# A transformer stack on one core: the first pass of attention scores fills two neighbouring PSUM banks, and one maximum reads both

## The chip, the cores and the metric

The kernel runs on one core of one Trainium2 chip. The metric is the device time of one execution in microseconds (us). Engines are named as in the profile: PE is TensorE (PEld its weight loads), DVE is VectorE, ACT is ScalarE, POOL is GpSimd and SP is SyncE, which issues most DMAs. PSUM is where PE leaves its results; this kernel treats it as eight banks of 512 float32 columns in 128 partitions.

## The reference

Four transformer layers run over 4 batches of 512 tokens with 288 channels. Each has 16 attention heads of width 18 and a feed-forward part of width 1152; layer 0 has four experts, with two chosen for each token. Cut to attention and the order of the layers:

```python
def _attention(h, W_qkv, b_qkv, W_proj, b_proj):
    qkv = h @ W_qkv + b_qkv
    q, k, v = ...                      # 16 heads of 18
    attn = softmax(einsum('blhd,bmhd->bhlm', q * scale, k), axis=-1)
    o = einsum('bhlm,bmhd->blhd', attn, v).reshape(b, l, c)
    return o @ W_proj + b_proj
...
x = x + gate_msa * _attention(modulate(layernorm(x)))
x = x + gate_mlp * mlp(modulate(layernorm(x)))
```

The softmax is computed against the maximum of each row of scores. So every score is computed twice: a first pass with queries in the rows, from which only the row maxima are kept, and a second pass with keys in the rows, into which the negated maxima enter as two more rows of the contraction.

## The kernel before

A planner (`plan`) writes one list of steps for all engines; each engine's program walks the list and executes its own part of every step. So the order of work on each engine is the order of the list. `pe[0]` is the planner's own clock: each `put` adds the estimate of its kind from `PE_NS` (a step `s1` counts 230), and side work is woven in when that clock has moved on by a set amount.

The list has 16 stages of attention (batch b of layer L is i = 4L + b), and the feed-forward part of stage i - 1 follows the attention of stage i. Layer 2 groups its attention another way (`s1b`, `s2b`), which the change does not touch. In the other twelve stages:

- `s1_steps(i)` is the first pass. For each of 8 head pairs p and 4 query tiles q it puts two steps `s1` (x = 0 and 1: one matmul each, weights from partitions 64x to 64x + 53, 512 key columns, into a bank of its own), then two steps `s1_max`, one DVE reduction per bank. That is 8 * 4 * 2 * 12 = 768 matmuls (line L1737) and 768 reductions (L1496). After every two head pairs `rows` turns the maxima (L1743), splits them on DVE (L1502, L1505) and stores them by DMA (L1111) for the second pass.
- `at_steps(i)` is the second pass. A step `s2` (L1750) fills a pair of banks (4 and 5, or 2 and 3) with two matmuls, and ACT reads each pair in one exponential of 1024 columns (L1345). `av` (L1760) multiplies with the values into bank 6.
- `s1_steps(i + 1)` is a stream. Part of it runs one call per step inside the attention of stage i, and the rest beside the feed-forward part, as a side of `weave`. Stage 0 has nothing to hide its own first pass behind: 16 head-pair tiles run before its first `s2`, and 2 or 1 more follow each later step until they are done.
- `mid(i)` is woven between the feed-forward tiles too: `turn_o` turns the attention output (three steps, L1693 and L1695; ACT copies it, then DVE takes the remainder, L1481 or L1484), `project` multiplies four token tiles (L1647 with weights WP; DVE reads the bank in L1571), and `turn_x` turns the normed rows (three steps, L1680 and L1682; ACT reads the bank twice or three times, DVE last in L1472 or L1475). `fc1` (L1856) and `fc2` (L1871) are the feed-forward matmuls and use banks 2, 3, 6 and 7, `hid` is the DVE part between them (L1626).

Banks. `ring()` hands out single banks in turn, from a tuple that depends on the place: `RING_A` = (0, 1, 7) in attention, `RING_B` = (0, 1, 4, 5) beside the feed-forward part, `RING_0` = (0, ..., 5) for a short while after the attention of stage 0. The steps `s1`, `rows`, `turn_o`, `turn_x`, `project`, the query and key projection and the turned output in attention all draw from the same ring. `pair(k)` claims banks k and k + 1 together. On PE `may_fill(bk, n)` waits until the earlier content of the bank has been read: it waits for a semaphore that the reader of the bank raises. If the bank belonged to a pair, it waits for the reader of the pair.

`weave` beside the feed-forward part: in layer 0 at most one `s1` tile per 5000 of the planner's clock; in the six stages i = 5, 6 and 11 to 14 one after 400, so one after nearly every feed-forward step (one `fc1` tile or two `fc2`), and `mid` steps after 800, so a turn or a projection between any two such tiles for as long as `mid` has steps.

Of the kernel before, what the change touches and what calls it, by code (L numbers as in the profile page):

```python
# [11 lines left out]
AX = mybir.AxisListType  # L12
# [43 lines left out]
def r(ap):  # L56
    return ap.bitcast(F32R)


def view(ap, part, free, dims):  # L60

    step = ap.ap[0][0]
    return bass.AP(ap.tensor, ap.offset + part * step + free,
                   [[s * step if isp else s, n] for s, n, isp in dims])
# [14 lines left out]
def plan(full, s_av, s_tn, s_fc2, s_qw):  # L79
# [8 lines left out]
    def put(*a):  # L88
        steps.append(a)
        pe[0] += PE_NS.get(a[0], 0)  # L90
# [20 lines left out]
    def bank(k):  # L111
        settle(k)
        fills[k] += 1
        if in_pair[k]:
            other[k, fills[k] - 1] = (k - 1, in_pair[k])
        return (k, fills[k] - 1)
# [10 lines left out]
    ring_of, ring_n = [RING_0], [0]  # L127

    def ring():
        ring_n[0] += 1  # L130
        return bank(ring_of[0][ring_n[0] % len(ring_of[0])])

    jobs = [("ada", 0, 0), ("q", 0), ("v", 0), ("ada", 0, 1), ("ada", 0, 2), ("wg",), ("p", 0)]
    jobs += [("f", k) for k in range(3)]
# [183 lines left out]
    n_qt, qw, qk_n = [0], [0, 0, 0], [0, 0, 0]  # L318
# [88 lines left out]
    def s1_steps(i):  # L407
        def rows(g, last):
            bk = ring()
            put("rows", i, g, bk, last, m2_wait[0])  # L410
            m_n[g] += 4 * 16
            m2_wait[0] = (g, m_n[g])
            mrow[g] = m_n[g]
            s1_at[0] = (i, g)

        late = None
        for p in range(H // 2):
            g = p // 2
            for q in range(QT):
                while not hurry[0] and pe[0] < qk_at.get((i, min(g, 2)), 1e9) + QK_LAND:  # L420
                    yield
                bks = []
                for x in range(2):
                    bk = ring()
                    put("s1", i, p, q, x, bk, qk_n[min(g, 2)])
                    bks.append(bk)
                for x in range(2):
                    put("s1_max", p, q, x, bks[x])
                yield
                if late is not None and q == DEFER:  # L430
                    rows(*late)
                    late = None
                    yield
            if p % 2:
                late = (g, bk)
        yield
        rows(*late)
        yield
# [339 lines left out]
    for i in range(NI + 1):  # L778
        L, b = i // 4, i % 4
        if i < NI:  # L780
# [41 lines left out]
            m = mid(i)  # L822
# [26 lines left out]
def build(nc, x_in, cond, layers, gate_w, out):  # L849
    ctx = ExitStack()  # L850
    with ctx:
# [21 lines left out]
        QS = sb("QS", [128, 8, T])  # L873
        KS = sb("KS", [128, 8, T])
# [19 lines left out]
        MX = [sb(f"MX{n}", [128, 16]) for n in range(2)]  # L894
# [11 lines left out]
        PSA = ctx.enter_context(nc.psum_tensor("PSA", [128, 8 * 512], F32))  # L906
# [478 lines left out]
        def dve_program(e):  # L1385
# [3 lines left out]
            for kind, *a in steps:  # L1389
                if kind == "fix":  # L1390
                    key, k, m = a
# [98 lines left out]
                    e.tensor_tensor(r(HH[u][0:M, 1, :]), PS[bk][0:M, :], HH[u][0:M, 0, :],  # L1490
                                    ALU.subtract).then_inc(free[bk], 1)
                elif kind == "s1_max":
                    p, q, x, (bk, n) = a
                    col = 8 * x + 4 * (p % 2) + q
                    w.wait_ge(full[bk], n + 1)
                    e.reduce_max(MX[p // 2 % 2][:, col:col + 1], PS[bk][:, :], axis=AX.X).then_inc(free[bk], 1)  # L1496
                elif kind == "rows":
                    i, g, (bk, n), _, old = a
                    if old is not None:
# [129 lines left out]
        def pe_program(e):  # L1629
# [21 lines left out]
            for kind, *a in steps:  # L1651
# [79 lines left out]
                    token_rows(A[i % 2], [WV[:, 0, :], WV[:, 1, :]], [WVL[:, 0, :], WVL[:, 1, :]],  # L1731
                               WV[:, 2, :], q, bk).then_inc(full[bk], 1)
                elif kind == "s1":
                    i, p, q, x, (bk, n), land = a
                    w.wait_ge(s_qk[min(p // 2, 2)], land)
                    may_fill(bk, n)
                    e.matmul(PS[bk][:, :], r(QS[64 * x:64 * x + 54, p, q * 128:(q + 1) * 128]),  # L1737
                             r(KS[64 * x:64 * x + 54, p, :]), start=True, stop=True).then_inc(full[bk], 1)
                elif kind == "rows":
                    i, g, (bk, n), last, _ = a  # L1740
                    w.wait_ge(free[last[0]], last[1] + 1)
# [185 lines left out]
```

## Time and profile before

| | us |
|---|---|
| median of 3 runs | 2257.18 |
| lowest and highest | 2246.01 and 2261.70 |
| span of the profiled execution | 2257.0 |
| PE busy, DVE busy, ACT busy in it | 2033.0, 1335.6, 1143.6 |

The span is the time from the first to the last instruction of one profiled execution. Busy time is time in which the engine has an instruction in work, however slowly it proceeds: two matmuls that overlap count once, and a matmul at half the clock counts at its longer duration. A group of instructions is named by its line in the kernel and by out<-in. "Idle before" is the idle time of an engine just before the instructions of the group, with the engine whose instruction ended it.

### The profile page before, as it was taken

The page shows a single profiled execution, that of the slowest core. Times are in us where ns is not written, and L with a number is a line of the kernel's source. Part 1 is how long each engine was busy: PE and PEld are TensorE (multiplying, and loading weights), DVE is VectorE, ACT ScalarE, POOL GpSimd, SP SyncE. Part 2 cuts the span into 40 slices and gives each one's busy share as a digit, 9 for nine tenths or more (in the row PEclk, how much of TensorE's full clock was granted, in tenths as well). Part 3 has the DMA queues.
Part 4 walks back from the last instruction along what each step waited for, and adds up shares of the span by engine and source line. Part 5 has one row for each costly group of instructions (what it writes and reads, how often), then busy time and mean ns, then how long its engine had stood idle before and what let it go on. Part 6 is the DMA issues. An engine that isn't in the chain of part 4 may idle for free.

```text
span 2257.0 us, 38969 instructions
## 1 busy us (share of the span) xinstructions
PE 2033.0 (90%) x15592; PEld 1509.0 (67%) x15592; DVE 1335.6 (59%) x2940; ACT 1143.6 (51%) x1705; POOL 207.4 (9%) x311
## 2 busy tenths in 40 slices
PE   6978899899989998999799899899888898999898
PEld 4347388658966994788375657788786556464658
DVE  4757637756774767476556673462444849484833
ACT  2444624574655456445626464552443464637373
POOL 2000001202100211012010000011000000000001
PEclk9787989899989999999889999998898998999999
DMA  5333332343333233333322313346254141314011
GB/s 158 77 123 57 100 95 72 79 111 86 89 77 106 72 89 76 96 94 88 94 72 35 103 17 65 73 88 109 34 95 130 7 121 26 99 11 115 9 14 25
DMA packets 204731, 173.97 MB, mean 77 GB/s; under 512 B 54822, under 2 KB 164678, under 8 KB 204550
## 3 DMA queue, kind: packets, MB, share of 16 engines
q1 hardware_dynamic: 197974, 158.76, 30.1%
q0 software_dynamic: 6576, 12.71, 2.1%
q8 instruction: 124, 2.03, 0.4%
q14 instruction: 57, 0.47, 0.1%
HBM read 125.57 MB, written 40.11 MB: 73 GB/s over the span
## 4 chain that ended last, share of the span: by engine, by line
PE 63%; DVE 18%; ACT 12%; DMA 3%; issue 2%; SPq 2%; POOL 0%; ACTq 0%; POOLq 0%; DVEq 0%
PE PSA L1856 16%; PE PSA L1871 13%; DVE MX L1496 7%; PE PSA L1647 5%; PE PSA L1760 5%; PE PSA L1737 5%; ACT PB L1345 4%; PE PSA L1707 4%; PE PSA L1750 4%; PE PSA L1719 2%; DVE FL L1396 2%; PE PSA L1780 1%; ACT FH L1375 1%; PE PSA L1670 1%; DVE HH L1626 1%
## 5 line engine op out<-in xcount | busy, mean ns | idle before, releaser
L1496 DVE TENSOR_REDUCE MX<-PSA 128x1 f32<-128x512 f32 x768 | 490.4, 682 | 296.9 <-PE PSA L1737 293.2
L1856 PE MATMUL PSA<-A,FH 128*128 128x256 f32 x2520 | 445.3, 292 | 12.5 <-DVE HH L1626 9.6
L1871 PE MATMUL PSA<-FH,HH 128*128 128x288 f32 x2016 | 447.7, 313 | 2.0 <-DVE HH L1626 2.0
L1382 ACT ACTIVATE HH<-PSA 128x512 fp32r<-128x512 f32 x252 | 150.4, 597 | 572.5 <-PE PSA L1856 567.3
L1345 ACT ACTIVATE PB<-PSA 128x1024 f32<-128x1024 f32 x384 | 370.9, 1025 | 102.5 <-PE PSA L1750 101.8
L1856 PEld LDWEIGHTS PSA<-A,FH 128*128 128x128 f32 x2520 | 364.9, 195 | 34.6 <-issue 17.3
L1871 PEld LDWEIGHTS PSA<-FH,HH 128*128 128x128 f32 x2016 | 329.7, 195 | 42.3 <-issue 38.0
L1871 PE MATMUL PSA<-FL,HH 128*128 128x288 f32 x1008 | 303.7, 301 | 0.0
L1737 PE MATMUL PSA<-KS,QS 54*128 54x512 f32 x768 | 226.1, 517 | 40.0 <-DVE MX L1496 14.0
L1255 POOL TENSOR_TENSOR X<-X,TM 128x288 f32<-128x288 f32 x128 | 101.1, 808 | 1496.7 <-DVE TM L1561 1496.6
L1760 PE MATMUL PSA<-PB,VT 128*32 128x512 f32 x1536 | 219.6, 637 | 0.0
L1750 PE MATMUL PSA<-QS,KS 56*128 56x512 f32 x768 | 172.6, 498 | 51.2 <-ACT PB L1345 27.2
L1626 DVE TENSOR_TENSOR HH<-PSA,HH 128x512 fp32r<-128x512 f32 x252 | 171.8, 682 | 76.1 <-ACT PSA L1383 75.8
L1856 PE MATMUL PSA<-A,FL 128*128 128x256 f32 x1008 | 208.0, 288 | 6.3 <-DVE FL L1396 6.3
L1871 PEld LDWEIGHTS PSA<-FL,HH 128*128 128x128 f32 x1008 | 196.8, 195 | 0.0
L1750 PEld LDWEIGHTS PSA<-QS,KS 56*128 56x128 f32 x768 | 70.2, 198 | 165.4 <-ACT PB L1345 84.8
L1737 PEld LDWEIGHTS PSA<-KS,QS 54*128 54x128 f32 x768 | 94.3, 203 | 115.1 <-DVE MX L1496 37.8
L1856 PEld LDWEIGHTS PSA<-A,FL 128*128 128x128 f32 x1008 | 159.3, 195 | 10.3 <-DVE FL L1396 9.1
L1383 ACT ACTIVATE PSA<-PSA 128x512 f32<-128x512 f32 x252 | 149.5, 593 | 0.0
L1375 ACT CAST FH<-ST 128x672 fp32r<-128x672 f32 x171 | 123.2, 748 | 32.9 <-PE PSA L1871 13.5
L1396 DVE TENSOR_TENSOR FL<-ST,FH 128x544 fp32r<-128x544 f32 x171 | 125.3, 733 | 5.3
L1707 PE MATMUL PSA<-A,WQ 128*126 128x512 f32 (+1 forms) x300 | 95.5, 421 | 23.0 <-DVE HH L1490 9.5
(166 smaller groups left out, 2261.5 us busy)
## 6 DMA issues: line engine op xcount, KB each, us to landing
qkd<-HH SPq DMA_DIRECT2D x48, 504.0 KB
ST<-in_L_cond_w SPq DMA_DIRECT2D x51, 432.0 KB
ST<-in_L_cond_w SPq DMA_DIRECT2D x102, 192.0 KB
QS<-qkd SPq DMA_DIRECT2D x88, 144.0 KB
KS<-qkd SPq DMA_DIRECT2D x88, 144.0 KB
QS<-qkd SPq DMA_DIRECT2D x144, 72.0 KB
KS<-qkd SPq DMA_DIRECT2D x144, 72.0 KB
ST<-in_L_cond_w SPq DMA_DIRECT2D x153, 48.0 KB
```

The costliest lines, as they stand in the source:

```text
L1345: e.activation(pbf[st % 3][:, p * 1024:(p + 1) * 1024], PSA[:, bk * 512:(bk + 2) * 512], ACT.Exp, scale=SCALE).then_inc(free[bk], 1)
L1382: e.activation(r(HH[u][:, 0, :]), PS[bk][:, :], gelu)
L1383: e.activation(PS[bk][:, :], PS[bk][:, :], gelu).then_inc(s_gelu, 1)
L1396: e.tensor_tensor(r(lo), ST[k % 2][:, s0:s0 + nl], hi[:, 0:nl], ALU.subtract).then_inc(s_wlo, 1)
L1496: e.reduce_max(MX[p // 2 % 2][:, col:col + 1], PS[bk][:, :], axis=AX.X).then_inc(free[bk], 1)
L1626: e.tensor_tensor(r(HH[u][:, 1, :]), PS[bk][:, :], HH[u][:, 0, :], ALU.subtract).then_inc(free[bk], 1)
L1707: m = e.matmul(PS[bk][0:M, :], r(w_), r(x_), start=(z == 0), stop=(z == 6))
L1737: e.matmul(PS[bk][:, :], r(QS[64 * x:64 * x + 54, p, q * 128:(q + 1) * 128]), r(KS[64 * x:64 * x + 54, p, :]), start=True, stop=True).then ...
L1750: m = e.matmul(PS[bk + x][:, :], r(KS[64 * x:64 * x + 56, 2 * g + p, kt * 128:(kt + 1) * 128]), r(QS[64 * x:64 * x + 56, 2 * g + p, :]), s ...
L1760: m = e.matmul(PS[bk][32 * hh:32 * hh + 32, :], VT[:, kt, h * V1:h * V1 + 32], PB[st % 3][:, hh, :], start=(kt == 0), stop=(kt == 3))
L1856: m = e.matmul(PS[bk][:, s_ * 256:(s_ + 1) * 256], r(w_), r(x_[:, half * 256:(half + 1) * 256]), start=(z == 0), stop=(z == 6))
L1871: m = e.matmul(PS[bk][:, 0:C], r(HH[u][:, c, tk]), r(w_), start=False, stop=(j == NCH - 1 and z == 2))
```

## The change

In `s1_steps` the two matmuls of a tile no longer draw two banks one by one. A new `ring_pair()` walks the same ring until it meets an even bank followed by its neighbour, and claims both as a pair. One step `s1` then issues both matmuls after one wait and raises one semaphore behind the second. One step `s1_max` waits for it and reduces 2 x 512 columns in one DVE instruction, which writes the two maxima 8 columns apart. The columns of MX, the matmuls themselves and everything behind `rows` are as before. The planner now counts one `s1` where it counted two.

```diff
+    def ring_pair():
+        order = ring_of[0]
+        while True:
+            ring_n[0] += 1
+            k, k1 = order[ring_n[0] % len(order)], order[(ring_n[0] + 1) % len(order)]
+            if k % 2 == 0 and k1 == k + 1:
+                ring_n[0] += 1
+                return pair(k)
...
-                bks = []
-                for x in range(2):
-                    bk = ring()
-                    put("s1", i, p, q, x, bk, qk_n[min(g, 2)])
-                    bks.append(bk)
-                for x in range(2):
-                    put("s1_max", p, q, x, bks[x])
+                bk = ring_pair()
+                put("s1", i, p, q, bk, qk_n[min(g, 2)])
+                put("s1_max", p, q, bk)
...
-                    p, q, x, (bk, n) = a
-                    col = 8 * x + 4 * (p % 2) + q
+                    p, q, (bk, n) = a
+                    col = 4 * (p % 2) + q
                     w.wait_ge(full[bk], n + 1)
-                    e.reduce_max(MX[p // 2 % 2][:, col:col + 1], PS[bk][:, :], axis=AX.X).then_inc(free[bk], 1)
+                    e.reduce_max(view(MX[p // 2 % 2][:, :], 0, col, [(1, 128, True), (8, 2, False)]),
+                                 PSA[:, bk * 512:(bk + 2) * 512].rearrange("p (x n) -> p x n", x=2),
+                                 axis=AX.X).then_inc(free[bk], 1)
...
-                    i, p, q, x, (bk, n), land = a
+                    i, p, q, (bk, n), land = a
                     w.wait_ge(s_qk[min(p // 2, 2)], land)
                     may_fill(bk, n)
-                    e.matmul(PS[bk][:, :], r(QS[64 * x:64 * x + 54, p, q * 128:(q + 1) * 128]),
-                             r(KS[64 * x:64 * x + 54, p, :]), start=True, stop=True).then_inc(full[bk], 1)
+                    for x in range(2):
+                        m = e.matmul(PS[bk + x][:, :], r(QS[64 * x:64 * x + 54, p, q * 128:(q + 1) * 128]),
+                                     r(KS[64 * x:64 * x + 54, p, :]), start=True, stop=True)
+                    m.then_inc(full[bk], 1)
```

## Rows read from the trace of the kernel before

**Rows 1.** The page: span, busy time by engine, the chain that ended last by line

```profile
span 2257.0 us, 38969 instructions
PE 2033.0 (90%) x15592; PEld 1509.0 (67%) x15592; DVE 1335.6 (59%) x2940; ACT 1143.6 (51%) x1705; POOL 207.4 (9%) x311
PE PSA L1856 16%; PE PSA L1871 13%; DVE MX L1496 7%; PE PSA L1647 5%; PE PSA L1760 5%; PE PSA L1737 5%; ACT PB L1345 4%; PE PSA L1707 4%; PE PSA L1750 4%; PE PSA L1719 2%; DVE FL L1396 2%; PE PSA L1780 1%; ACT FH L1375 1%; PE PSA L1670 1%; DVE HH L1626 1%
```

**Rows 2.** The page's groups: busy us, mean ns | idle before, what ended it

```profile
L1496 DVE TENSOR_REDUCE MX<-PSA 128x1 f32<-128x512 f32 x768 | 490.4, 682 | 296.9 <-PE PSA L1737 293.2
L1345 ACT ACTIVATE PB<-PSA 128x1024 f32<-128x1024 f32 x384 | 370.9, 1025 | 102.5 <-PE PSA L1750 101.8
L1737 PE MATMUL PSA<-KS,QS 54*128 54x512 f32 x768 | 226.1, 517 | 40.0 <-DVE MX L1496 14.0
```

**Rows 3.** Idle PE and PEld before L1737, 0 to 200 us, by releaser (us, times)

```profile
  DVE MX L1496: 35.0, 62
```

**Rows 4.** The same from 200 us to the end

```profile
  DVE A L1472: 21.7, 25
  DVE MX L1496: 16.8, 26
  DVE A L1481: 16.5, 20
```

**Rows 5.** Busy time by stretch: PE, PEld, DVE, ACT, POOL; granted clock, DMA share, GB/s

```profile
50.00:62.00 12.00, 11.64 (x21) 5.40 (x21) 11.20 (x19) 0.00 (x0) 0.00 (x0) 0.50 0.70 202
```

**Rows 6.** Timeline of stage 0's first pass, half clock: start, length, instructions [idle before]

```profile
49.97 0.80 PE L1737 MATMUL PSA<-KS,QS 54*128 54x512 f32 x2 [3.35 <-DMA KS<-qkd]
...
50.80 12.05 DVE L1496 TENSOR_REDUCE MX<-PSA 128x1 f32<-128x512 f32 x20 [3.92 <-PE PSA L1737]
...
68.87 1.54 PE L1750 MATMUL PSA<-QS,KS 56*128 56x512 f32 x4
...
73.87 1.94 PE L1760 MATMUL PSA<-PB,VT 128*32 128x512 f32 x8
```

**Rows 7.** Timeline at full clock: a step with two tiles, then a tile alone

```profile
92.08 2.48 DVE L1496 TENSOR_REDUCE MX<-PSA 128x1 f32<-128x512 f32 x4
92.82 0.49 PE L1737 MATMUL PSA<-KS,QS 54*128 54x512 f32 x1 [0.76 <-DVE MX L1496]
93.24 1.06 PE L1760 MATMUL PSA<-PB,VT 128*32 128x512 f32 x8
...
153.70 0.50 PE L1737 MATMUL PSA<-KS,QS 54*128 54x512 f32 x2
```

**Rows 8.** Groups by shape on DVE: one operation at two lengths

```profile
L1396 DVE TENSOR_TENSOR FL<-ST,FH 128x544 fp32r<-128x544 f32 x171 | 125.3, 733 | 5.3
...
L1396 DVE TENSOR_TENSOR WQL<-ST,WQ 128x1152 fp32r<-128x1152 f32 x4 | 5.4, 1359 | 0.1
```

**Rows 9.** L1737 in the last of six dense stretches: PE, PEld, clock, DMA share, GB/s

```profile
2077.00:2135.00 58.00, 12.30 (x42) 4.74 (x42) 0.98 0.20 35
```

**Rows 10.** Timeline: projection, tile, maxima, next projection, DVE's read of the first

```profile
1863.57 0.69 PE L1647 MATMUL PSA<-WP,A 128*128 128x288 f32 x4
...
1864.58 0.51 PE L1737 MATMUL PSA<-KS,QS 54*128 54x512 f32 x2
...
1865.12 1.29 DVE L1496 TENSOR_REDUCE MX<-PSA 128x1 f32<-128x512 f32 x2 [0.47 <-PE PSA L1737]
...
1865.91 0.69 PE L1647 MATMUL PSA<-WP,A 128*128 128x288 f32 x4
...
1866.33 0.45 DVE L1571 TENSOR_TENSOR TD<-PSA,GB 128x288 f32<-128x288 f32 x1
```

**Rows 11.** Timeline: two turns of the attention output, and the tile behind the second

```profile
1850.68 0.60 PE L1693 MATMUL PSA<-ID,OT 128*128 128x128 f32 x4
1851.48 0.68 DVE L1481 TENSOR_TENSOR A<-PSA,A 128x512 fp32r<-128x512 f32 x1
1852.22 0.50 PE L1737 MATMUL PSA<-KS,QS 54*128 54x512 f32 x2 [0.94 <-DVE A L1481]
```

## The prediction

> **What bounds the kernel now.** I read the page first: busy times and the chain that ended last [rows 1]. PE is busy 2033.0 of 2257.0 us and DVE 1335.6, and the feed-forward lines L1856 and L1871 lead the chain. DVE's maxima still stand there with 7%. Then the groups [rows 2]: the 768 maxima cost DVE 490.4 us, and of the idle time of PE before the score matmuls (40.0 us) 14.0 us end with a maximum. So DVE as a whole is not the bound, and I have to see where PE waits for it. I asked the line L1737 for its releasers in two stretches. These counts add idle time of PE and of its weight loads, so they show where and not how much. Before 200 us maxima account for 35.0 us [rows 3]. In all the rest, more than 2000 us, they account for 16.8, and there the larger part is waits for reads of turned tiles (L1472 and L1481, 21.7 and 16.5) [rows 4]: a score matmul drew a bank that a turn had used just before. So two places matter: stage 0, whose own first pass hides behind nothing, and the six dense stages of the feed-forward part (i = 5, 6, 11 to 14), where tiles, turns and projections share one ring; the last of them is in [rows 9].
>
> **The price of one maximum.** The trace has no reduction over 1024 columns. The bound from below is the one over 512, 0.68 us [rows 2], and from above two of them, 1.36. One DVE operation at 544 and 1152 elements takes 0.733 and 1.359 us, 1.03 ns for each further element [rows 8]; so I take 0.682 + 512 * 0.00103 = 1.21 us. ACT's read of a pair points the same way: a single 1.025 us instruction reads two banks [rows 2]. Busy DVE time falls by 384 * (1.36 - 1.21) = 58 us. Where reductions follow each other they start 12.05 / 20 = 0.60 us apart [rows 6], so what DVE saves in its queue is 1.20 - (0.60 + 0.53) = 0.07 us per tile, not 0.15.
>
> **The price of one fill.** Two score matmuls use different halves of the rows and run side by side when both banks are free: two take 0.80 us at half clock [rows 6] and 0.50 us at full clock [rows 7], where one alone takes 0.49 [rows 7]. So issuing them together costs PE nothing, and it is what PE already does after 200 us.
>
> **The banks.** Here the change costs. RING_A = (0, 1, 7) holds only one even pair, so every tile in attention gets banks 0 and 1. The next tile cannot start until the maximum over both has ended. Three single banks become one buffer.
>
> *Stage 0, 16 tiles before the first s2.* They run at half the clock, 0.50 granted [rows 5]. Before, DVE is the bound at 2 * 0.60 = 1.20 us per tile, and the last fill is followed by s2 at 68.87 [rows 6]. After, a tile is a closed loop: 0.06 us from the release to the matmul (the first of four maxima ends at 92.76, the matmul starts at 92.82 [rows 7]), 0.80 for the fill, 0.03 to the start of the reduction (50.77 to 50.80 [rows 6]), 1.21: 2.10 us. Fifteen loops from 49.97 put s2 at 49.97 + 31.5 = 81.5 instead of 68.9: **+12.7 us**. Behind that s2 stand two tiles, s2, rows, one tile and av, which came 5.00 us after s2 [rows 6]. Now three loops (6.3) and 0.7 for the fill: **+2.0**.
>
> *Stage 0, five more steps with two tiles each.* The second tile waits for the maximum of the first: 92.08 + 1.21 + 0.06 = 93.35, and av follows 0.42 later as before, at 93.77 instead of 93.24 [rows 7]; 5 * 0.53 = **+2.7**. Nothing hides these 17 us. PE, DVE and then s2, ACT and av work in series there, and behind PE's waiting score matmul stand s2, av and the projections of the next stage. The SP queue is delayed with them, since its weight loads wait for DVE's splits, which stand in the same list.
>
> *Attention of later stages:* one tile per step. The loop at full clock is 0.06 + 0.50 + 0.03 + 1.21 = 1.80 us, and a step has two exponentials of 1.025 us [rows 2], so it fits: 0. The cover is ACT and PE together; gone, it would cost what stage 0 pays.
>
> *The dense stages.* RING_B = (0, 1, 4, 5) has two pairs, so tiles alone alternate and stay double-buffered. With a turn or projection between two tiles that ends. It takes, say, bank 4; ring_pair skips 5 and takes 0 and 1; the next single bank is 4 again. So each turn or projection waits for the read of the one before it, where until now they went round four banks. A projection starts at 1863.57, its tile 1.01 later, the maximum 0.54 after that, and DVE reads the projection (0.45 us, L1571) only behind the maximum, since its step comes later in the list [rows 10]. With 1.13 for the maximum in the queue and 0.06 to PE, the next one can start 1.01 + 0.54 + 1.13 + 0.45 + 0.06 = 3.19 us after the first. It started 2.34 after [rows 10]: +0.85. A stage has four such steps (three between projections, one to the rows step), one of them with a long fc1 between, which I count at half: 3.5 * 0.85 = 3.0. In the turns the wait exists already, one place later: the tile behind the second turn waits 0.94 us for L1481 [rows 11]. Now the turn itself would wait until 1851.48 + 0.68 + 0.06 = 1852.22, when the tile used to start; the tile comes one turn (0.60) later: +0.6, twice: 1.2. The turns of normed rows move in the same way, and there the waits of the tiles for L1472 fall away; I count 0 and bound it by another 1.2. A stage costs 3.0 + 1.2 = 4.2, six stages **+25**. From below it is 0, if DVE comes so much earlier that the next one is ready; from above 6 * 5.4 = 32.
>
> *The rest.* Layer 0's sparse stages have a long fc1 or four fc2 between such steps: 0. After the attention of stage 0 RING_0 has three pairs and DVE is the bound; by the code some 17 tiles * 0.07 = **-1**. In the dense stages DVE's backlog shrinks; what PE waits for maxima there is inside the 16.8 [rows 4], I take **-6** of it. The planner's clock, which counts a tile at 230 instead of 460, moves side work by at most a step or two: 0.
>
> A rule of the Trainium skill speaks for the change. VectorE: DVE Perf Modes, section on the TRN2 errata, says that a fixed latency is paid per instruction, so that "a single large tile pays it once". By the figures of its table (120 cycles plus the columns at 0.96 GHz) an estimate is 0.66 us for 512 columns and 1.19 for 1024. The trace agrees for the first (0.68); no run here shows the second.
>
> **The sum.** 2257.0 + 12.7 + 2.0 + 2.7 + 25 - 1 - 6 = 2292 us. The span of the profiled execution is the median of the runs (2257.18), so I leave it at that.
>
> **The rivals.**
> 1. *Only stage 0 pays.* The shared single bank in the dense stages is paid back by DVE's shorter queue. For: the last of these stretches has 42 score matmuls, 21 tiles, in 58 us [rows 9], so there is air between them. Against: the arithmetic of rows 10. Time: 2257 + 17 - 1 - 3 = 2270.
> 2. *Faster, or not slower: the DVE saving counts on the path.* Maxima are 7% of the chain, 158 us [rows 1]; at 1.21 instead of 1.36 that is 11% less, -17: 2240. For: the chain. Against: in stage 0, where these 7% mostly lie, the loop decides. It turns at a loop of 1.20 us; with 0.89 for release, fill and start the reduction would have to take 0.31, less than one over 512 columns. The skill's rule above is this rival.
> 3. *The clock falls more often.* The first pass of stage 0 ran at half clock with PE waiting between single fills [rows 5]. If the new short waits in the dense stages bring that state there, the fc1 and fc2 work of a few stretches takes twice its time; at 3 more us for each of the six stages on top of the forecast, 2292 + 18 = 2310. TensorE: Matmul & The Clock Gate, section on PSUM-queue depth-cycling, describes such a fall when PE idles briefly between groups of matmuls. The last dense stage, with 0.98 granted in spite of its waits [rows 9], speaks against it.
>
> **How the numbers follow.** Forecast (both places pay) 0.60, rival 1 0.22, rival 2 0.06, rival 3 0.12. The forecast's own range is 2277 to 2304: stage 0 between 13 and 20, dense stages between 12 and 32. The range for 8 in 10 reaches to rival 1 and rival 3: 2264 to 2314. One per cent is 22.6 us, about what a measurement of this kernel can tell from no change. Over 2279.8 lie rival 3 and nine tenths of the forecast, 0.66; rival 1, the rest of the forecast and most of rival 2 lie within 1%, 0.31; faster 0.03.
>
> **What the profile after would show.** The maximum as x384 at about 1210 ns. In stage 0 fills about 2.1 us apart, with PE waiting for MX, and the first s2 near 81.5 us. L1750 and L1760 shifted by 17 at the end of that attention. In the dense stages waits of L1647 for L1571 and of L1693 for L1481, which are not there now, and fewer waits of L1737 for L1481. Wrong I would be if the dense stages ran through as before (rival 1), if the reduction over two banks took under 1 us, or if something in stage 0 turned out to wait for a DMA that lands at the same time in both kernels.

## The result, and the profile after

| | before | after |
|---|---|---|
| median, us | 2259.44 | 2380.39 |
| lowest and highest | 2246.01 and 2262.40 | 2371.58 and 2382.43 |
| span of the profiled execution | 2257.0 | 2369.8 |

The changed kernel takes 1.054 times as long (95% interval 1.051 to 1.058): 121 us more, where 35 were forecast and 57 was the upper end of the range. The direction was right, the size off by more than three times.

Lines of the kernel after: the maximum is L1501 (L1496 before), the first-pass matmul L1745 (L1737), `rows` L1752 (L1743) with its DMA in L1116 (L1111), the second pass L1759 (L1750), `av` L1769 (L1760), the exponential L1350 (L1345), the projection L1654 (L1647) with its DVE reads in L1568 and L1578 (L1561, L1571), `turn_o` L1700 and L1702 with its DVE read in L1486, `turn_x` L1687 and L1689 with its DVE read in L1477, `fc1` L1865, `hid` L1633.

The page of the kernel after, the lines that answer to [rows 1] and [rows 2]:

```profile
span 2369.8 us, 38586 instructions
PE 2038.3 (86%) x15592; PEld 1501.3 (63%) x15592; DVE 1314.4 (55%) x2556; ACT 1147.0 (48%) x1705; POOL 207.3 (9%) x311
...
L1501 DVE TENSOR_REDUCE MX<-PSA 128x2 f32<-128x1024 f32 x384 | 467.8, 1220 | 344.7 <-PE PSA L1745 344.0
L1745 PE MATMUL PSA<-KS,QS 54*128 54x512 f32 x768 | 201.6, 521 | 72.9 <-DVE MX L1501 47.6
```

One maximum takes 1.220 us (1.21 forecast). DVE works 21 us less than before, PE 5 us more. Of the 113 us of span 107 are more idle time of PE. But the 5 us are the difference of two larger changes. The first-pass matmuls, which now always run side by side, fill 24.5 us less of PE's time (226.1 [rows 2] and 201.6). All its other instructions are the same as before and take longer: the time in which PE is busy with one of them is 1866 us before and 1892 after. The granted clock has two levels in both traces, 0.5 and 1.0. Its mean is 0.932 before and 0.917 after, and the time at 0.5 is 309 and 394 us. So some 25 us of the loss are work that takes longer, as it does at the lower clock, and the rest are waits. The trace of waits (idle time of PE in all, times, longest) names those, and they aren't in one place:

```profile
PE PSA L1745 <- DVE MX L1501: 47.6, 43, 2.9
PE PSA L1759 <- ACT PB L1350: 35.0, 38, 5.4
PE PSA L1759 <- DMA QS<-M: 18.3, 6, 6.0
PE PSA L1687 <- DVE A L1477: 14.7, 10, 2.6
PE PSA L1759 <- DVE MX L1501: 14.3, 8, 2.9
...
PE PSA L1654 <- DVE TD L1578: 10.2, 15, 1.6
```

Besides the waits for maxima there are two kinds that the forecast did not price where they came: the second pass of stage 0 waits for a DMA (`QS<-M`, the stored row maxima), and turns and projections wait for DVE's reads of the turn or projection before them.

Stage 0's first pass, from the timeline of PE (start, length, instructions, idle before): the fills, and the first `s2`.

```profile
79.97 0.80 PE L1745 MATMUL PSA<-KS,QS 54*128 54x512 f32 x2 [1.32 <-DVE MX L1501]
82.08 0.79 PE L1745 MATMUL PSA<-KS,QS 54*128 54x512 f32 x2 [1.32 <-DVE MX L1501]
82.67 1.06 PE L1759 MATMUL PSA<-QS,KS 56*128 56x512 f32 x4
```

Fills start 2.11 us apart (2.10 forecast), and the first `s2` stands at 82.67 instead of 68.87 [rows 6] (81.5 forecast). Then come the rows of the second and third group (PE's turn, its DMA on the SP queue, and the `s2` that needs it):

```profile
98.81 0.38 PE L1752 MATMUL PSA<-ID,MX 128*16 128x128 f32 x1
...
99.92 2.67 SPq L1116 DMA_DIRECT2D QS<-M  x4
...
105.23 1.22 PE L1759 MATMUL PSA<-QS,KS 56*128 56x512 f32 x4 [6.04 <-DMA QS<-M]
...
125.63 0.38 PE L1752 MATMUL PSA<-ID,MX 128*16 128x128 f32 x1
...
130.58 1.22 PE L1759 MATMUL PSA<-QS,KS 56*128 56x512 f32 x4 [4.57 <-DMA QS<-M]
```

From the turn to the `s2` it takes 6.4 and 5.0 us, and PE idles through 6.04 and 4.57 of it. In the kernel before, PE had other work between the two.

I split the 113 us at the first `s2` of each stage and at the first value projection behind its attention, so the attention of a stage and the feed-forward part beside it stand apart. Each kernel has one profiled execution. Two kernels that differ before the first `s2` alone (those of experiments 4 and 5) are up to 5 us apart in one of the later places, so a few us in one place say little. After less before, in us:

| | first `s2` | attention 0 | sparse: beside feed-forward of layer 0 (i = 1 to 4) | attention of 3 and 4 | dense: i = 5, 6, 11 to 14 | all the rest |
|---|---|---|---|---|---|---|
| forecast | 12.7 | 4.7 | 0 | 0 | 25 - 6 = 19 | -1 |
| measured | 13.8 | 23.0 | 34.2 | 11.1 | 22.9 | 7.8 |

The first and the dense part came near the forecast. 68 us came where the forecast had 4.7, 0 and 0. The time at half the clock grew from 41 to 85 us up to the end of attention 0 and from 35 to 64 us in the sparse stages; in the dense ones it was 63 us before and 55 after.

### The profile page after: what moved, and what is told of

Its sections match the earlier page's. It is cut to its first block, busy times and chain, and to the rows that moved or that the text cites. A ratio compares the mean times of both kernels' runs of the same rounds, so it can differ in the third digit from the quotient of the medians.

```text
span 2369.8 us, 38586 instructions
## 1 busy us (share of the span) xinstructions
PE 2038.3 (86%) x15592; PEld 1501.3 (63%) x15592; DVE 1314.4 (55%) x2556; ACT 1147.0 (48%) x1705; POOL 207.3 (9%) x311
## 4 chain that ended last, share of the span: by engine, by line
PE 59%; DVE 20%; ACT 13%; issue 3%; DMA 3%; SPq 2%; POOL 0%; ACTq 0%; POOLq 0%; DVEq 0%
PE PSA L1865 15%; PE PSA L1880 11%; DVE MX L1501 8%; PE PSA L1769 6%; PE PSA L1654 5%; PE PSA L1745 4%; PE PSA L1759 4%; PE PSA L1714 4%; ACT PB L1350 3%; DVE FL L1401 2%; ACT FH L1380 2%; PE PSA L1726 2%; DVE HH L1633 2%; PE PSA L1789 1%; ACT HH L1387 1%
## 5 line engine op out<-in xcount | busy, mean ns | idle before, releaser
L1501 DVE TENSOR_REDUCE MX<-PSA 128x2 f32<-128x1024 f32 x384 | 467.8, 1220 | 344.7 <-PE PSA L1745 344.0
L1865 PE MATMUL PSA<-A,FH 128*128 128x256 f32 x2520 | 447.7, 293 | 22.7 <-DVE HH L1633 12.5
L1350 ACT ACTIVATE PB<-PSA 128x1024 f32<-128x1024 f32 x384 | 370.5, 1023 | 143.8 <-PE PSA L1759 143.0
L1865 PEld LDWEIGHTS PSA<-A,FH 128*128 128x128 f32 x2520 | 366.1, 196 | 47.0 <-issue 21.7
L1745 PE MATMUL PSA<-KS,QS 54*128 54x512 f32 x768 | 201.6, 521 | 72.9 <-DVE MX L1501 47.6
L1759 PE MATMUL PSA<-QS,KS 56*128 56x512 f32 x768 | 175.1, 511 | 73.9 <-ACT PB L1350 35.0
L1769 PE MATMUL PSA<-PB,VT 128*32 128x512 f32 x1536 | 226.3, 654 | 0.3 <-ACT PB L1350 0.3
L1633 DVE TENSOR_TENSOR HH<-PSA,HH 128x512 fp32r<-128x512 f32 x252 | 171.7, 681 | 97.5 <-ACT PSA L1388 97.2
L1865 PE MATMUL PSA<-A,FL 128*128 128x256 f32 x1008 | 208.8, 289 | 5.2 <-DVE FL L1401 5.0
L1759 PEld LDWEIGHTS PSA<-QS,KS 56*128 56x128 f32 x768 | 70.9, 204 | 191.6 <-ACT PB L1350 87.5
L1745 PEld LDWEIGHTS PSA<-KS,QS 54*128 54x128 f32 x768 | 80.4, 205 | 139.8 <-DVE MX L1501 64.8
L1865 PEld LDWEIGHTS PSA<-A,FL 128*128 128x128 f32 x1008 | 160.0, 196 | 9.0 <-DVE FL L1401 8.0
L1380 ACT CAST FH<-ST 128x672 fp32r<-128x672 f32 x171 | 123.0, 748 | 24.5 <-PE PSA L1880 14.3
L1714 PE MATMUL PSA<-A,WQ 128*126 128x512 f32 (+1 forms) x300 | 95.7, 422 | 19.9 <-DVE HH L1495 8.2
```

Source lines behind the costliest of these rows:

```text
L1350: e.activation(pbf[st % 3][:, p * 1024:(p + 1) * 1024], PSA[:, bk * 512:(bk + 2) * 512], ACT.Exp, scale=SCALE).then_inc(free[bk], 1)
L1380: e.copy(r(hi), ST[k % 2][:, s0:s0 + nh]).then_inc(s_whi, 1)
L1501: e.reduce_max(view(MX[p // 2 % 2][:, :], 0, col, [(1, 128, True), (8, 2, False)]), PSA[:, bk * 512:(bk + 2) * 512].rearrange("p (x n) -> ...
L1633: e.tensor_tensor(r(HH[u][:, 1, :]), PS[bk][:, :], HH[u][:, 0, :], ALU.subtract).then_inc(free[bk], 1)
L1714: m = e.matmul(PS[bk][0:M, :], r(w_), r(x_), start=(z == 0), stop=(z == 6))
L1745: m = e.matmul(PS[bk + x][:, :], r(QS[64 * x:64 * x + 54, p, q * 128:(q + 1) * 128]), r(KS[64 * x:64 * x + 54, p, :]), start=True, stop=True)
```

## The experiments

In every one of them, "restored" or "halved" is the entry of a step `s1` in `PE_NS`, the planner's estimates. The kernel before takes between 2255.6 and 2259.4 us in all comparisons. Numbers for places are differences to the execution of [rows 1], divided as in the table above.

**1. The planner's clock alone, both ways.** A tile was two steps of 230 on the planner's clock and is now one of 230. One kernel is the changed one with the old cost per tile, the other is the kernel before with the new one.

```diff
 # the changed kernel:
-         "s1": 230,
+         "s1": 460,
```

> The changed kernel with the planner's count of a tile set back to its old sum (an s1 step counts 460, not 230), so that all work stands in the order of the kernel before and only the banks, the one semaphore and the one maximum are changed. Banks theory (the closed loop over one pair and turns and projections that fall on the same bank cost the time, the order costs nothing): as the changed kernel, 2370 to 2385. Clock theory (halving the count moved steps, above all the rows steps of stage 0, so that PE waits for their DMAs): the 16 us of waits of L1759 for QS<-M in stage 0's attention go and some of the waits in the sparse stages; 2340 to 2355 if it is half of the loss above my forecast, under 2300 if it is nearly all.

```diff
 # the kernel before:
-         "s1": 230,
+         "s1": 115,
```

> The kernel before with an s1 step counted 115 instead of 230, so a tile counts 230 as in the changed kernel: the order of work of the changed kernel, with the banks and maxima of before. Clock theory: slower by what the order costs, 15 to 40 us, with PE waiting for DMA QS<-M about 6 us twice in stage 0. Banks theory: within 5 us of before. If the two parts add, this run's loss and that of the run with the count restored sum to the 121 us of the change.

Measured: 2344.04 us with the clock restored (ratio 1.037, 1.034 to 1.040), 85 us over the kernel before. The clock alone: 2295.86 us (1.016, 1.013 to 1.019), 37 us over it. The two add up to 122, and the change cost 121. So the banks and the single maximum cost 85, and a number that no engine ever sees costs 37. With the clock alone, attention 0 is 21.9 us longer and the sparse stages 2, 3 and 4 lose 3.6, 6.4 and 2.9. The wait is the same as in the changed kernel:

```profile
109.91 0.28 PE L1743 MATMUL PSA<-ID,MX 128*16 128x128 f32 x1
...
115.68 1.22 PE L1750 MATMUL PSA<-QS,KS 56*128 56x512 f32 x4 [5.49 <-DMA QS<-M]
```

**2. Why the clock costs so much in stage 0.** `s1_steps` starts with a gate: the tiles of a group are not listed before the planner's clock has passed the time at which the group's queries and keys were asked for, by `QK_LAND` = 12000.

```python
                while not hurry[0] and pe[0] < qk_at.get((i, min(g, 2)), 1e9) + QK_LAND:
                    yield
```

With tiles at half the cost the planner's clock passes this mark later. In its list the first three steps of attention 0 get no tile, and the rows of the second and third group stand right ahead of the first `s2` of their group; in the kernel before two more steps of the attention lie between. The kernel here is the clock alone (as above), and stage 0 has no gate.

```diff
-                while not hurry[0] and pe[0] < ...
+                while i and not hurry[0] and pe[0] < ...
```

> The run with the clock alone changed, without the gate that holds back tiles of stage 0 until the planner's clock has passed a mark. Clock theory: the 21 us that stage 0's attention costs there come from this gate alone (tiles skipped in three steps, then rows steps right before the s2 that needs them), so they go: about 2275. What stays, 15 us in the sparse stages 2 to 4, comes from the places of turns and projections. If it stays at 2296, the gate is not the cause.

Measured: 2270.46 us (1.0075, 1.0046 to 1.0104), 25 us less than with the gate by the medians and 19 by the two ratios, and the waits of PE for `QS<-M` are 2.6 us in all (19.2 with the gate, 3.3 in the kernel before). Attention 0 takes 67.0 us, where it took 92.8 with the gate and 70.9 in the kernel before: the 21.9 us that the clock costs there are gone, and 4 more with them. So the gate in stage 0 is some 22 of the 37 us. (The kernel before without the gate was not run, so how much of the 4 us is this edit by itself is open.) The rest, about 15, stays in this kernel too, 10.5 of it in the sparse stages 2 to 4; which of the moved turns and projections makes it was not tried.

**3. The choice of banks alone.** The kernel before with its two semaphores and its two maxima, but the two banks of a tile are an even one and its neighbour, found by the same walk as `ring_pair`.

```diff
-                for x in range(2):
-                    bk = ring()
+                for x, k in enumerate(ring_two()):
+                    bk = bank(k)
```

> The kernel before, with its order, its two semaphores and its two maxima, but the two banks of a tile always drawn as an even bank and its neighbour, as the changed kernel draws them. Turns and projections then fall on the same bank as in the changed kernel, but each bank comes free by itself. If the shared bank of turns and projections is the cost, this is near the run with the clock restored, less only the longer loop of stage 0: there the loop per tile should be 0.06 + 0.80 + 0.03 + 0.68 = 1.57 us instead of 2.10, so 15 * 0.5 = 8 us and some 5 us in the steps with two tiles less. If the single maximum and semaphore are the cost, it is near before (2259).

Measured: 2355.82 us (1.042, 1.037 to 1.046), 97 us over the kernel before. The first `s2` is 3.8 us late and not 11.6, because here the next tile's first matmul waits for one maximum only. In attention 0, the sparse stages and attention 3 and 4 it is within 2 us of the changed kernel with the clock restored; it is worse in the dense stages (44 us lost against 32) and in all the rest (9 against -1). So the whole of the 85 us comes with the banks that a tile may take, and merging semaphore and maximum gives some 12 us back.

**4. The bank that has rested longest.** The changed kernel, clock restored, and both `ring` and `ring_pair` take the bank, or the pair, that was drawn longest ago, in place of the next one of the tuple.

```diff
-        return bank(ring_of[0][ring_n[0] % len(ring_of[0])])
+        k = min(ring_of[0], key=lambda k: (used[k], ring_of[0].index(k)))
+        used[k] = ring_n[0]
+        return bank(k)
...
-        while True:
-            ring_n[0] += 1
-            k, k1 = order[ring_n[0] % len(order)], order[(ring_n[0] + 1) % len(order)]
-            if k % 2 == 0 and k1 == k + 1:
-                ring_n[0] += 1
-                return pair(k)
+        k = min((k for k in order if k % 2 == 0 and k + 1 in order),
+                key=lambda k: max(used[k], used[k + 1]))
+        used[k] = used[k + 1] = ring_n[0]
+        return pair(k)
```

> The run with the clock restored, but single banks and pairs are drawn by longest time since use instead of by walking the ring, so that turns and projections alternate between two banks while tiles stay on the other pair. In attention nothing changes: tiles still have only banks 0 and 1. If the collisions of turns and projections are the cost outside stage 0, this falls to 2257 + 17 for stage 0 - 7 for DVE = about 2267, at most 2275. If it stays where the run with the clock restored is, the collisions are not the cost.

Measured: 2267.47 us (1.0036, 1.0019 to 1.0053). 77 of the 85 us are gone, with the same pairs and the same single maximum. Stage 0 has lost 20.3 us. Behind it every sparse and dense stage is faster than before or at most 2 us slower (the last three are faster by 3 to 5 us), and attention 3 and 4 are within 2. The waits of PE's projections for DVE's reads of the projection before (`TD`, 10.7 us with the clock restored) and of its turns for those of the turned attention output (14.7 us) are gone from the list. The planner's list shows why. In stage 2 the three turns and four projections draw banks 5, 4, 1, 0, 1, 0, 5 in the kernel before, 0, 0, 0, 0, 1, 0, 0 in the changed one with its clock restored, and 5, 4, 5, 4, 5, 4, 5 here. What is left is stage 0, where `RING_A` has one pair, whatever is chosen:

```profile
PE PSA L1747 <- DVE MX L1503: 49.5, 47, 2.3
```

**5. Three pairs for stage 0's first pass.** Banks 2 to 5 are idle until the first `s2`; a tile listed before it may take them.

```diff
-        order = ring_of[0]
+        order = ring_of[0] if s2_first[0] else RING_0
...
+                s2_first[0] = True          # at the first s2
```

> The run with least recently used banks, and until the first s2 of stage 0 the tiles may also use the pairs 2-3 and 4-5, which are idle then. Banks theory: the closed loop over one pair costs 12 us there; with three pairs DVE is the bound at 0.60 + 0.53 = 1.13 us per tile, the first s2 comes at 50 + 16 * 1.13 + 1 = 69 us instead of 81, and the total falls by 12 to about 2255. If the single reduction or the half clock were the cost there, the first s2 stays near 81.

Measured: 2254.83 us (0.9995, 0.9974 to 1.0016), 13 us less than the run before (9 by the two ratios). The first `s2` comes at 66.33 us (69 expected, 68.87 in the kernel before). On the timelines of PE and DVE tiles now start 1.13 us apart, and DVE is what they wait for:

```profile
52.18 0.80 PE L1749 MATMUL PSA<-KS,QS 54*128 54x512 f32 x2 [0.34 <-DVE MX L1505]
53.31 0.79 PE L1749 MATMUL PSA<-KS,QS 54*128 54x512 f32 x2 [0.34 <-DVE MX L1505]
...
48.63 11.41 DVE L1505 TENSOR_REDUCE MX<-PSA 128x2 f32<-128x1024 f32 x10 [1.62 <-PE PSA L1749]
```

Ten maxima in 11.41 us: 1.14 each, where ten tiles before took 12.05 [rows 6].

**6. The second tile behind `av`.** Where a step of attention 0 has two tiles, they share one pair, so `av` stood behind a matmul that waits for a maximum. The second tile now goes behind `av`.

```diff
-            for _ in range(2 if i == 0 else 1):
-                s1_step()
+            s1_step()
...
+            if i == 0 and st < 16:
+                s1_step()                   # behind av
```

> The run before, and in the attention of stage 0 the second tile of a step stands behind av instead of right behind the first, so that av's matmuls cover the maximum of the first tile. Banks theory: the wait of 1.3 us of the second tile (seven such steps) goes, 5 to 9 us less than the run with the wide first pass, about 2248, below the kernel before. If something else holds stage 0's steps (ACT, the DMAs of rows), no change against that run.

Measured: 2246.33 us (0.9959, 0.9939 to 0.998), 9 us under the kernel before in the same comparison. It is the fastest of all. Attention 0 takes 71.7 us, where it took 80.9 in the run before and 70.9 in the kernel before. Not all of these 9 us are the waits: in attention 0 the clock is at half for 17 us, against 38 in the run before, and PE is busy 7.7 us less with the same matmuls.

**7. What the single maximum is worth.** Two more kernels go back to two semaphores and two maxima of 512 columns, the banks still drawn as pairs that rested longest: once in the kernel before, and once with all placements of the fastest one.

> The kernel before with the banks drawn as in the run with least recently used banks (same order, same banks), but two semaphores and two maxima per tile. It tells what the single maximum gives when the banks are the same: by my count 0.07 us per tile wherever DVE is behind, so this is slower than the run with least recently used banks by 5 to 15 us in the dense stages, and faster by some 8 to 12 us in stage 0, where each bank comes free by itself; total 2262 to 2275.

> The kernel of the later second tile and the least recent banks, but each first-pass tile again with two semaphores and two maxima of 512 columns in place of one of 1024. Theory A (the single maximum itself is worth something where VectorE is the one behind): the 384 maxima cost 1.22 us each against 2 x 0.66 us, 0.10 us a tile, so at most 38 us of VectorE's time, of which the path sees a part: 2250 to 2262 us. Theory B (the placements and the bank choice made the whole gain, and the maximum nothing): 2246 us, as the kernel with the single maximum.

Measured: 2270.05 us (1.0058, 1.0033 to 1.0082), and 2260.20 us (1.0001, 0.9981 to 1.002). With the same order and banks as the fastest kernel, two maxima cost more than one: 14 us by the medians, 9 by the two ratios, each ratio uncertain by 4 to 5 us. Experiment 3 against the changed kernel with its clock restored gives 12. The first of the two kernels against experiment 4 gives only 3 (5 by the two ratios): two maxima are 11 us slower in the dense stages, but the first `s2` comes 7 us earlier, since there each bank comes free by itself, both near what was expected. So one semaphore and one maximum together are worth 3 to 14 us, by the kernel that they stand in, and 9 to 14 in the fastest. In the single executions of the two fastest kernels the difference sits in stage 0 (the first `s2` 2 us, its attention 1.6, the stretch behind it 3.5) and in the dense stages 12 to 14 (about 6), and the sparse stages go 4 us the other way. A part of it is the granted clock, which is at half for 284 us with one maximum and for 318 with two. What one maximum gives at the same clock was not separated.

**8. Are the reads late because they are listed late?** In the sparse stages of the changed kernel PE waits before turns and projections, though long `fc1` and `fc2` work stands between them. In stage 2 (540.5 to 708.6 us of the kernel after), the waits of PE:

```profile
...
PE PSA L1700 <- DVE A L1486: 2.7, 1, 2.7
PE PSA L1687 <- DVE A L1477: 2.5, 1, 2.5
PE PSA L1654 <- DVE TM L1568: 2.1, 1, 2.1
```

The last of them on the timeline: the projection is complete in its bank before 567, DVE reads it at 572.79, and the next projection starts 0.05 us after this read has ended.

```profile
566.22 0.30 PE L1654 MATMUL PSA<-WP,A 98*128 98x288 f32 x1
...
570.23 1.23 DVE L1501 TENSOR_REDUCE MX<-PSA 128x2 f32<-128x1024 f32 x1 [4.24 <-PE PSA L1745]
571.37 0.93 DVE L1568 SCALAR_TENSOR_TENSOR TM<-PSA,CW,GB 128x288 f32<-128x288 f32 x2
572.79 0.46 DVE L1568 SCALAR_TENSOR_TENSOR TM<-PSA,GB 128x288 f32<-128x288 f32 x1 [0.48 <-POOL X L1260]
...
573.30 1.33 PE L1654 MATMUL PSA<-WP,A 128*128 128x288 f32 x4 [2.13 <-DVE TM L1568]
```

In the code these reads are put with `later(...)`: they enter the list only when `mid` is taken up again, or when the bank is drawn again. That is right ahead of the next turn or projection, behind all the `hid` and maxima between. DVE was not busy all that time: it stood idle for 4.24 us ahead of the maximum that comes before the read in its list. The kernel with the clock restored, and the reads listed directly behind their matmuls:

```diff
-            later(bk[0], put, "turno_lo", c, slot, bk, n_o[0])
+            put("turno_lo", c, slot, bk, n_o[0])
...
-            later(bk[0], residual, i, q, bk, 0)
+            residual(i, q, bk, 0)
```

(and the same in both forms of `turn_x`)

> The changed kernel with the cost of the planner's clock restored, and with the VectorE and ScalarE reads of turns and projections listed directly behind their matmuls, not when the attention's chain is taken up again. Theory A (a read listed late makes the next turn or projection, which has the same bank, wait for it, whatever stands between): the sparse stages' 20 us of loss and a part of the dense ones' go, 2310 to 2330 us against 2344 us. Theory B (the read is slow in itself, and where it is listed changes nothing): 2344 us. Theory C (a read listed at once holds back the maxima or the copies behind it on VectorE and ScalarE): over 2350 us.

Measured: 2306.78 us (1.021, 1.018 to 1.025), 37 us less (36 by the two ratios). The sparse stages' loss goes from 19.9 to 5.2 us, the dense ones' from 32.2 to 13.1. In stage 2 PE no longer waits before a turn or a projection. But the same edit could be good by itself, so it was made in the kernel before and in the fastest kernel, where banks go round.

> The kernel before with the reads of turns and projections listed directly behind their matmuls, as the control of the same edit in the changed kernel, where it gave 37 us. Theory A (the late listing costs only together with the shared bank): within 6 us of the kernel before, 2252 to 2265 us. Theory B (it costs in any kernel of this shape): 2215 to 2235 us, and the 37 us then say nothing about the shared bank.

> The fastest kernel so far (least recent banks, wide first pass, second tile later) with the reads of turns and projections listed directly behind their matmuls. Theory A (a late listing costs only where the next turn or projection has the same bank): here the banks rotate, so nothing is to be had, 2244 to 2250 us against 2246 us. Theory B (a late listing costs by itself): some 15 to 35 us less, 2210 to 2232 us. Theory C (a read listed at once holds back the maxima behind it, and the rotation makes it needless): 2250 to 2265 us.

Measured: 2264.08 us (1.0033, 1.0009 to 1.0056) for the kernel before with it, 7 us more than without, and 2273.11 us (1.0071, 1.0046 to 1.0096) for the fastest with it, 27 us more than without (25 by the two ratios); that is more than any theory had. The late listing is right where banks rotate: it keeps DVE's list free for `hid`, on which `fc1` waits. In the fastest kernel with the edit that wait is

```profile
PE PSA L1870 <- DVE HH L1638: 23.0, 20, 2.9
```

where without the edit it is 9.3 us in 14 waits. DVE, too, now stands idle behind ACT's copy of a turn (L1491 behind L1321) for 118.0 us in all, against 10.0 without. These two waits are the largest that grew; that they make up the 25 us is not shown. So 37 us less with the shared bank, and 7 and some 25 us more without it: the late listing costs only together with the bank that returns at once.

## Why the prediction was wrong

**Right: the parts that were worked out from rows.** The maximum 1.22 us (1.21). The closed loop 2.11 us (2.10), the first `s2` 13.8 us late (12.7). The rule on one large tile in the Trainium skill (VectorE: DVE Perf Modes, section on the TRN2 errata) leads to an estimate of 1.19 us from its table; the trace has 1.22 and so agrees. (The sentence quoted there is about operands in SBUF. What bears on a maximum over PSUM is the table, which has a fixed 120 cycles for a read from PSUM.) It is also true that the saving is worth time, 9 to 14 us in the fastest kernel of experiment 7, but only once the bank is no longer the bound. The dense stages: the mechanism is the one forecast, at 25 us less 6 for DVE's shorter queue, 19; measured 22.9 in the changed kernel and 32.2 with the clock restored, which is above the 32 - 6 = 26 that the prediction's upper bound comes to. The waits that it named are there (L1654 for L1578, 10.2 us; L1700 and L1702 for L1486, 3.9 and 6.1 us). Side by side the two matmuls of a tile took 0.80 us at half the clock, as [rows 6] had them, also when one semaphore covers both.

**Wrong, step 1: "The planner's clock ... moves side work by at most a step or two: 0".** It cost 37 us (experiment 1), some 22 of them through one gate in stage 0 (experiment 2). The count of steps was about right: three steps of attention 0 get no tile. What was not asked is what stands behind a moved tile. Here it is the `rows` step: a turn on PE, a split on DVE, a DMA and its landing, 5.0 to 6.4 us in series, and an `s2` at the end of them. A step of 230 can be moved for nothing, the last tile of a group cannot.

**Wrong, step 2: "Layer 0's sparse stages have a long fc1 or four fc2 between such steps: 0".** They lost 19.9 us with the clock restored (34.2 in the changed kernel, the planner's clock included). The argument was that distance hides the read. It doesn't: the read is listed where the next turn is listed, so the distance from read to next fill is near zero however much work stands between the two fills. With another bank for the next fill that is harmless. With the same bank PE waits each time until DVE has come to this place in its list, even where DVE is idle on the way. Experiment 8 shows both halves. A part of the 19.9 is slower work behind the waits: PE is busy 598 us there and not 587, with 55 us at half the clock and not 35. The dense stages have late reads too (19 of their 32 us go in experiment 8), so 3.5 * 0.85 and 1.2 were small for the same reason.

**Wrong, step 3: "Attention of later stages ... it fits: 0".** Attention 3 and 4 lost 5.8 and 6.0 us with the clock restored; the other nine of the stages behind stage 0 that the change touches lost under 2 us together. What is late in these two stages is not settled: the longest new wait of stage 3 there is an `s2` behind a DVE read of the residual (L1568, 2.4 us), and no single wait makes up 6 us. They run within 2 us of before once banks rotate (experiment 4), so the loss comes with the choice of banks; listing the reads of turns and projections at once did not help (5.8 and 7.4), so it isn't their late listing. The reads of the query and key projections are put with `later(...)` too and draw from the same ring; experiment 8 left them as they were, so they are an untested candidate.

**Wrong by a part: the rest of stage 0.** Forecast 4.7 us behind the first `s2`; with the clock restored it is 9.8, with the gate's part 23.0. The two terms, 2.0 and 2.7, were the loops. Most of what is missing to the 9.8 is in the rows of attention 0, before and with the clock restored (busy PE, PEld, DVE, ACT, POOL; granted clock, DMA share, GB/s):

```profile
68.90:139.80 70.90, 61.49 (x317) 27.45 (x317) 42.30 (x96) 42.94 (x54) 4.08 (x7) 0.86 0.28 73
...
80.50:161.30 80.80, 66.20 (x317) 27.34 (x314) 40.97 (x77) 42.74 (x54) 4.09 (x7) 0.75 0.21 63
```

The same 317 matmuls keep PE busy 4.7 us longer. The clock is at half for 41 of 81 us, before for 19 of 71. So to the waits of the loop comes slower work, which the prediction had in rival 3 for the dense stages alone. That the waits bring the lower clock is argued and not shown. Over all kernels here the two go together in attention 0: the clock is at half for 14 to 26 us where it lost under 3 us, for 34 to 36 where it lost 5 to 6, and for 37 to 57 where it lost 9 or more.

**Wrong without a share in the sum.** Busy DVE time was to fall by 58 us. It fell by 23 for the maxima (490.4 [rows 2] to 467.8): the 58 took each reduction at its 0.68 us, though the prediction itself had read that queued ones start 0.60 apart. And the 7% of the chain that are maxima do not mostly lie in stage 0: of 163 us only 34 lie before 200 us.

**The rivals.** Rival 1 (only stage 0 pays) is wrong, both other places pay. Rival 2's mechanism is real and 3 to 14 us large, under its 17; but it needs banks, and in the changed kernel the loop decides in stage 0, as was said. Rival 3 (the clock falls more often) is wrong for the dense stages, where it was put: the time at half the clock went from 63 to 55 us. But the clock did fall more often elsewhere, in stage 0 and the sparse stages, and some 25 us of the loss are work that took longer with it. It came with the waits and no run holds it fixed, so it stands inside the terms above and not beside them.

All three failed steps carry the price 0, and none had a bound other than 0. Together they are 37 + 20 + 12 = 69 us of the 86 that were missing; 13 more are the dense stages (32 for 19), and 5 the attention of stage 0.

## What to carry to other kernels

A constraint on alignment is a change of buffer count: before two buffers are taken as one pair, count how many such pairs each ring has (here 1 of 3 banks and 2 of 4), and where singles and pairs share a ring, choose by the time since the last use and not by the next index. Where a reader is listed only when its buffer is wanted again, the distance between two fills hides nothing, so every return of the same buffer is a wait. And a constant that feeds a planner is an edit to the order of everything behind it: price it by what the last moved item of each group releases, a DMA first of all.

## What the runs showed of the hardware

A DVE maximum over two banks (1024 float32 columns from PSUM) takes 1.220 us and back to back 1.14; over one bank 0.68 and 0.60 [rows 2, 6]. So two single ones in a row, 1.20, lose only 0.06 us to one double, which is 23 us for the 384 tiles if DVE were behind in all of them; 3 to 14 us were measured, in three pairs of kernels.

Two matmuls of 54 rows, on partitions 0 to 53 and 64 to 117, run side by side into two banks in 0.80 us at half the clock and 0.50 at full, where one alone takes 0.49 [rows 7]. The Trainium skill (TensorEngine Tiling (Array Packing), section on PSUM pressure) says that different row tiles write to different banks. The runs agree in that every such pair here does, and they show the price of it: the pair is only side by side while both banks are free. From 50 to 62 us, at 0.50 granted, 21 such matmuls keep PE busy for 11.64 us in the kernel before, where each waits for its own bank [rows 5], and for 8.26 us in the fastest kernel.

The granted clock goes with the waits over the kernels: 309 us at half in the kernel before, 394 in the changed one, 353 with the planner's clock restored, 325 with rotating banks, 284 in the fastest. Where a placement took waits out of stage 0 (experiments 5 to 6), PE's busy time for the same work there fell by 7.7 us as well.

The path from a turned row maximum on PE to the second pass that reads it (a turn, DVE's split, four DMAs that the SP queue issues in 2.67 us, their landing) took 6.4, 5.0 and 5.8 us in three places of two kernels where PE waited for it.
